# Two queues for the loads of the pairs' results, and the last four tiles in two groups

## The reference

```python
x = x + 0.5 * ffn(layernorm(x), Wg, W1, b1, W2, b2)
x = x + attn(layernorm(x), Wq, bq, Wk, bk, Wv, bv, Wo, bo)     # linear attention, 16 heads of 8
x = x + 0.5 * ffn(layernorm(x), Wg, W1, b1, W2, b2)

def ffn(x):                       # 8 experts, top 2 of them for each row
    top_w, top_i = top_k(x @ Wg, 2);  top_w = softmax(top_w)
    for i in range(8):
        out_i = gelu(x @ W1[i] + b1[i]) @ W2[i] + b2[i]        # 128 -> 512 -> 128
        results += w_per_expert[..., i:i+1] * out_i
```

## Time and profile before

| | us |
|---|---|
| median of 3 runs | 366.19 |
| lowest and highest of the 3 | 363.96, 366.23 |
| profiled execution | 364.38 |
| its span, first to last instruction | 362.6 |
| busy: PE, DVE, ACT, POOL | 306.7, 205.2, 148.7, 193.9 |
| mean granted clock of TensorE, 1 is 2.4 GHz | 0.928 |

### The profile page before, as it was taken

The page is one execution under the profiler, slowest core; times in us unless marked ns, Lnnn a source line. Parts: engine busy times, 40 slices in busy tenths (PEclk is TensorE's granted clock), DMA queues, the critical chain, the costliest instruction groups (busy, mean ns, idle before and its releaser), DMA issues.

```text
span 362.6 us, 7860 instructions
## 1 busy us (share of the span) xinstructions
PE 306.7 (85%) x2040; PEld 253.7 (70%) x2047; DVE 205.2 (57%) x562; ACT 148.7 (41%) x480; POOL 193.9 (53%) x246
## 2 busy tenths in 40 slices
PE   8589898759789995899999995895997777599985
PEld 6355898749779964566777763464997767499844
DVE  2974463333245516799999999972553242345413
ACT  3652675433244321434554552822764342343200
POOL 9307556656645531676677773236556656555500
PEclk9766999998889999999999998589999899989997
DMA  6937575534446126000000000226574535354146
GB/s 208 314 118 197 151 195 147 157 106 132 131 123 185 60 67 196 0 0 2 1 3 0 1 3 30 89 67 173 153 212 130 164 101 157 102 166 136 43 128 228
DMA packets 23557, 41.52 MB, mean 114 GB/s; under 512 B 4065, under 2 KB 6113, under 8 KB 23522
## 3 DMA queue, kind: packets, MB, share of 16 engines
q1 hardware_dynamic: 19426, 32.68, 31.6%
q0 software_dynamic: 4096, 8.40, 7.8%
HBM read 33.72 MB, written 7.34 MB: 113 GB/s over the span
## 4 chain that ended last, share of the span: by engine, by line
PE 48%; DVE 18%; another core or an unknown queue 12%; issue 5%; DMA 5%; ACT 5%; POOL 3%; DVEq 2%; SPq 0%; POOLq 0%; ACTq 0%
PE banks L1120 16%; PE banks L1129 14%; PE banks L1252 4%; DMA y_back<-y_rows 3%; DVE prod L967 2%; DVE local L971 2%; PE banks L1082 2%; PE banks L1138 2%; DMA y_rows<-y_back,pair_row 2%; PE banks L1228 2%; PE banks L1020 2%; ACT h_act L583 1%; POOL kv L464 1%; PE banks L1192 1%
## 5 line engine op out<-in xcount | busy, mean ns | idle before, releaser
L887 DVE TENSOR_TENSOR h_pre<-banks,w1b 128x512 f32<-128x512 f32 x78 | 53.7, 689 | 80.2 <-PE banks L1120 59.1
L433 POOL DMA_INDIRECT y_back<-xn_rows,src_row x64 | 61.9, 968 | 66.7 <-issue 20.3
L1120 PE MATMUL banks<-rows_sb,w1b 128*128 x624 | 88.6, 287 | 0.9 <-issue 0.6
L1129 PE MATMUL banks<-w,h_act 128*128 x624 | 85.6, 284 | 0.0
L441 POOL DMA_INDIRECT y_rows<-y_back,pair_row x64 | 62.6, 978 | 39.0 <-DVE y_back L899 27.9
L1120 PEld LDWEIGHTS banks<-rows_sb,w1b 128*128 128x128 f32 x624 | 79.8, 200 | 3.9 <-issue 2.0
L1129 PEld LDWEIGHTS banks<-w,h_act 128*128 128x128 f32 x624 | 79.7, 201 | 0.0
L583 ACT ACTIVATE h_act<-h_pre 128x512 f32<-128x512 f32 x78 | 48.8, 625 | 21.8 <-DVE h_pre L887 20.5
L575 ACT COPY rows_sb<-banks 128x128 f32<-128x128 f32 x64 | 16.7, 261 | 86.4 <-remote 57.4
L899 DVE SCALAR_TENSOR_TENSOR y_back<-banks,own_item,y_back 128x128 f32 x78 | 27.4, 351 | 34.0 <-PE banks L1129 18.0
L1138 PE MATMUL banks<-ident,y_back 128*128 128x128 f32 x64 | 18.7, 292 | 29.8 <-ACT rows_sb L575 25.3
(11 more groups left out here) (214 smaller groups left out, 426.1 us busy)
## 6 DMA issues: line engine op xcount, KB each, us to landing
w1b<-in_W1b SPq DMA_DIRECT2D x78, 258.0 KB
y_back<-y_rows SPq DMA_DIRECT2D x16, 256.0 KB, 5.3
xn_rows<-rows_sb SPq DMA_DIRECT2D x8, 256.0 KB, 2.6
rows_sb<-in_x_T SPq DMA_DIRECT2D x4, 256.0 KB, 3.7
x<-in_x_tiles SPq DMA_DIRECT2D x4, 256.0 KB, 6.1
y_back<-xn_rows,src_row POOLq DMA_INDIRECT x64
y_rows<-y_back,pair_row POOLq DMA_INDIRECT x64
out<-x SPq DMA_DIRECT2D x4, 256.0 KB, 2.4
```

The source lines that it names most:

```text
L433: g.indirect_dma_start(out=xg[:, n, :], out_offset=None, in_=xn_rows[f][:, :], in_offset=bass.IndirectOffsetOnAxis(ap=src_row[:, n:n + 1], ...
L887: v.tensor_tensor(h_pre[:, r, :].rearrange("p (c n) -> p c n", c=FC), h_bank(r).rearrange("p (c n) -> p c n", c=FC), w1b[:, q, DF:DF + FC] ...
L1120: last = mm(h_bank(r)[:, c * P:(c + 1) * P], w1b[:, q, c * P:(c + 1) * P], xgT[:, bass.ds(at[i][0], P)], start=True, stop=True)
L1129: last = mm(y_bank(r), h_act[:, r, c * P:(c + 1) * P], w2[:, bass.ds(col + c * P, P)], start=(c == 0), stop=(c == FC - 1))
```

## The change

The four k = 0 loads of a loop stay on SP; the four k = 1 loads are issued by ScalarE, which waits for `scattered` itself. In loop 1 the last group of four tiles (t = 12 to 15) becomes two groups of two tiles, each with a bank of its own (3 and 4), its own two loads of 128 KB, its own `mix` on TensorE, its own wait on VectorE and its own store of 128 KB. Loop 0 keeps its four groups. In the diff stand, one behind the other, the tables, the loads on SP, the stores, ScalarE's loads at the end of its `ffn(f)`, VectorE's `combine(f)` and TensorE's `mix_b2` and `mix`.

```diff
+    FOURS = tuple((c * CH, (c + 1) * CH) for c in range(NC))
+    GROUPS = (FOURS, (*FOURS[:-1], (NT - CH, NT - 2), (NT - 2, NT)))
...
-        def mix_bank(c): return banks[:, (1, 2, 0, 3)[c], :]
+        def mix_bank(c): return banks[:, (1, 2, 0, 3, 4)[c], :]
...
+        def loads(f, c):
+
+            return 16 * (f + 1 if c < NC else 1)
...
-                for c in range(NC):
-                    for k in range(TOPK):
-                        sp.dma_start(y_back[:, k, c * CH:(c + 1) * CH, :],
-                                     back_rows[k, :, c * CH:(c + 1) * CH, :]).then_inc(y_loaded[k][c], 16)
+                for c, (a, b) in enumerate(GROUPS[f]):
+                    sp.dma_start(y_back[:, 0, a:b, :], back_rows[0, :, a:b, :]).then_inc(y_loaded[0][c], 16)
...
-            for c in range(NC):
-                sp.wait_ge(x_final, CH * (c + 1))
-                sp.dma_start(out_v[:, c * CH:(c + 1) * CH, :], x[:, c * CH:(c + 1) * CH, :]).then_inc(out_stored, 16)
-            sp.wait_ge(out_stored, 16 * NC)
+            for a, b in GROUPS[1]:
+                sp.wait_ge(x_final, b)
+                sp.dma_start(out_v[:, a:b, :], x[:, a:b, :]).then_inc(out_stored, 16)
+            sp.wait_ge(out_stored, 16 * len(GROUPS[1]))
...
+                act.wait_ge(scattered, 16 * NL * (f + 1))
+                back_rows = y_rows[f].rearrange("(k p t) d -> k p t d", k=TOPK, p=P)
+                for c, (a, b) in enumerate(GROUPS[f]):
+                    act.dma_start(y_back[:, 1, a:b, :], back_rows[1, :, a:b, :]).then_inc(y_loaded[1][c], 16)
...
-                for c in range(NC):
+                for c, (a, b) in enumerate(GROUPS[f]):
                     dve.wait_ge(mix_ps, NC * f + c + 1)
-                    dve.wait_ge(y_loaded[1][c], 16 * (f + 1))
-                    for t in range(c * CH, (c + 1) * CH):
+                    dve.wait_ge(y_loaded[1][c], loads(f, c))
+                    for t in range(a, b):
...
+            def mix_b2(f, c):
+
+                a, b = GROUPS[f][c]
+                four = a // CH
+                rows = slice(four * CH * E, (four + 1) * CH * E)
+                mm(mix_bank(c)[:, 0:(b - a) * P], w_allT[rows, :], b2_blk[rows, (a % CH) * P:(a % CH + b - a) * P],
                    start=False, stop=False, skip_group_check=True)
 
             def mix(f, c):
-                pe.wait_ge(y_loaded[0][c], 16 * (f + 1))
-                for t in range(c * CH, (c + 1) * CH):
+                a, b = GROUPS[f][c]
+                pe.wait_ge(y_loaded[0][c], loads(f, c))
+                for t in range(a, b):
```

More of the change, by code:

```diff
@@ L259, in macaron_kernel @@
         y_ps, y_sb = map(sem, ("y_ps", "y_sb"))
-        y_loaded = [[sem(f"y_loaded{k}_{c}") for c in range(NC)] for k in range(TOPK)]
+        y_loaded = [[sem(f"y_loaded{k}_{c}") for c in range(len(GROUPS[1]))] for k in range(TOPK)]
         xa_sb, xa_ps, xaT_sb, qkv_ps = map(sem, ("xa_sb", "xa_ps", "xaT_sb", "qkv_ps"))
@@ L932, in moments_2 @@
                         v.bn_stats(stats[:, t, :], x[:, t, :]).then_inc(stats_ready, 1)
-                for c in range(NC):
+                for c, (a, b) in enumerate(GROUPS[f]):
                     dve.wait_ge(mix_ps, NC * f + c + 1)
-                    dve.wait_ge(y_loaded[1][c], 16 * (f + 1))
-                    for t in range(c * CH, (c + 1) * CH):
+                    dve.wait_ge(y_loaded[1][c], loads(f, c))
+                    for t in range(a, b):
                         v.scalar_tensor_tensor(out=x[:, t, :], in0=y_back[:, 1, t, :], scalar=half_w[:, 1, t:t + 1],
-                                               in1=mix_bank(c)[:, (t % CH) * P:(t % CH + 1) * P],
+                                               in1=mix_bank(c)[:, (t - a) * P:(t - a + 1) * P],
                                                op0=ALU.mult, op1=ALU.add).then_inc(x_final if f else x_mid, 1)
@@ L1093, in experts @@
                 pe.wait_ge(table_ready, f + 1)
-                mix_x(0)
+                mix_x(f, 0)
                 keep_warm(WARM_EXPERTS)
@@ L1169, in experts @@
                     pe.wait_ge(b2_in, 16)
[L1170 to L1173, removed]
+                mix_b2(f, 0)
+                for c in range(1, len(GROUPS[f])):
+                    mix_x(f, c)
+                    mix_b2(f, c)
                 pe.wait_ge(y_sb, base + NS)
@@ L1176, in experts, with mix_x @@
                 pe.wait_ge(diag_ready, NT * (f + 1))
-            def mix_x(c):
-                for t in range(c * CH, (c + 1) * CH):
[L1181 to L1186, removed]
+            def mix_x(f, c):
+                a, b = GROUPS[f][c]
+                for t in range(a, b):
+                    mm(mix_bank(c)[:, (t - a) * P:(t - a + 1) * P], ident[:, :], x[:, t, :],
+                       start=(t == a), stop=False, skip_group_check=True)
+            def mix_b2(f, c):
[3 more added lines that the diff above has]
+                mm(mix_bank(c)[:, 0:(b - a) * P], w_allT[rows, :], b2_blk[rows, (a % CH) * P:(a % CH + b - a) * P],
                    start=False, stop=False, skip_group_check=True)
             def mix(f, c):
-                pe.wait_ge(y_loaded[0][c], 16 * (f + 1))
-                for t in range(c * CH, (c + 1) * CH):
-                    last = mm(mix_bank(c)[:, (t % CH) * P:(t % CH + 1) * P], diag[:, t, :], y_back[:, 0, t, :],
+                a, b = GROUPS[f][c]
+                pe.wait_ge(y_loaded[0][c], loads(f, c))
+                for t in range(a, b):
+                    last = mm(mix_bank(c)[:, (t - a) * P:(t - a + 1) * P], diag[:, t, :], y_back[:, 0, t, :],
                               start=False, stop=True, skip_group_check=True)
@@ L1298, in _ @@
             experts(1)
-            for c in range(NC):
+            for c in range(len(GROUPS[1])):
                 mix(1, c)
```

## The result

The first measurement: 372.46 us for the changed kernel (370.9 to 375.29, 4 runs) against 366.21 (363.96 to 369.37, 4 runs). The ratio on record is 1.0227, 95% interval 1.0175 to 1.028; it is formed from fast runs alone and is not the quotient of the two medians, which is 1.017. So the change measured slower by about 2%, where 365.0 us and a range up to 367.2 had been forecast. The profiled execution took 375.29 us, its span is 373.5, the mean granted clock 0.895 (before: 364.38, 362.6, 0.928).

A forecast was written before the change was run, and what follows sets the result against it. Bound: result loads, on the chain twice with nothing beside them to fill the time. Terms +0.3 + 0.1 - 0.1 - 0.4 = -0.1 us, applied to the four executions' mean 365.2 and rounded, gave 365.0 us; range 361.8 to 367.2.

The forecast's parts named there:

- The loads' landings: Sign, loop 0: a pair landing together at 4.0 to 4.7 us after issue confirms that the queues share the service.
- Loop 0, +0.3 us with bounds -0.6 and +1.1: First pair in loop 0: both loads land together, TensorE's part stands uncovered, VectorE starts group 0 0.3 us later.
- Rival 1: Loads in both loops: the second queue speeds the service, -0.5 to -1.7 us, down to -2.2, about 363.0 us; chance 0.27.
- The end, +0.1 -0.1 -0.4: End of loop 1: group 2's pair order +0.1 us, last group in two -0.1, half-size last store -0.4.
- TensorE's clock in the last three groups: Sign at the end of loop 1, listed without a size; rival 1 said TensorE perhaps stays at full clock.
- The sum of -0.1 us: Whole program: +0.3 + 0.1 - 0.1 - 0.4 = -0.1 us, within -0.6 to +0.4; chance 0.45.
- rival 2: Group 0 in loop 0, group 2 at the end: TensorE's cover lost, nothing won, +0.5 to +1.4 us, about 365.3; chance 0.18.
- TensorE ahead of the loads: Last group's bias matmul, split in two halves: same sum, weight loads at worst 0.3 us, 0.49 us waiting to spare: no cost.
- slower by over 1% has no mechanism here: 0.02: Whole program: nothing in the change could slow it by over 1%; chance 0.02, against 0.86 for within 1%.
- shifts elsewhere, in TensorE's clock or in the gathers: Outside the changed places: shifts said to move the time by less than 1%; chance 0.02 together with rival 4.
- rival 4: ScalarE's issue, loop 0: late at its wait, k = 1 loads follow k = 0; each microsecond late costs one; chance shared, 0.02.

The follow-up runs named there:

- e9: The changed kernel without an edit, repeated in the third job: 326.0 us, ratio 0.999 to the kernel before.
- e10: The kernel before without an edit, in the third job: 325.85 us, ratio 0.9991.
- e8: The changed kernel without an edit, repeated in the second job: 326.25 us, ratio 1.0017 to the kernel before.
- e4: The kernel before without an edit, in the first job of the experiments: 363.38 us, ratio 0.9974.
- e18: The kernel before without an edit, in the fifth job: 325.47 us, ratio 1.0009.
- e1: The changed kernel without an edit, in the first job of the experiments: 364.84 us, ratio 1.0025 to the kernel before.
- e13: The changed kernel without an edit, in the fourth job: 326.62 us, ratio 0.9995 to the kernel before.
- e17: The changed kernel without an edit, in the fifth job: 325.59 us, ratio 0.9993 to the kernel before.
- e5: Changed kernel; in loop 1 TensorE also waits for five ScalarE copies between its last item and first bias matmul: 334.51 us, ratio 1.0294 to the kernel before.
- e6: Kernel before with the added TensorE wait of e5: 332.98 us, ratio 1.0231 to the kernel before.
- e14: e5 again, the changed kernel with the added wait, in a later job: 332.68 us, ratio 1.0234 to the kernel before.
- e16: Kernel before with only the second load queue (four groups of four in both loops), plus the wait of e5: 334.36 us, ratio 1.0252.
- e15: e6 again, the kernel before with the added wait, in a later job: 334.11 us, ratio 1.0238 to the kernel before.
- e7: e5 with twelve bf16 matmuls on zeros behind the added wait: 329.72 us, ratio 1.0138 to the kernel before.

## Why the prediction was wrong, point by point

**The loads' landings: right.** Forecast was a pair that lands together at 4.0 to 4.7 us. Measured 4.1 and 4.3, in e9 4.0 and 4.2 (loop 0) and 4.2 and 4.4 (loop 1). On one queue the first load alone was sooner. The first load of loop 1 in e10, then the first pair of loop 1 in e9:

```profile
y_back<-y_rows SPq DMA_DIRECT2D x1, 256.0 KB, 3.2
...
y_back<-y_rows SPq DMA_DIRECT2D x1, 256.0 KB, 4.2
y_back<-y_rows ACTq DMA_DIRECT2D x1, 256.0 KB, 4.4
```

**Loop 0, +0.3 us with bounds -0.6 and +1.1: right.** VectorE's first sum started 5.3 to 5.7 us after the first issue in the 13 traces with two queues, median 5.5, and 4.7 to 6.0 us in the 7 with one, median 5.2. That is +0.3 or +0.4. Single traces could not have told it: on one queue they differ by more than that among themselves.

**Rival 1, faster service with two queues (0.27): did not come.** Slow windows like those of the earlier trace rows are there with two queues too. Windows of e9 behind the first issue:

```profile
310.38:311.38 1.00, 1.00 (x7) 0.73 (x6) 0.00 (x0) 0.00 (x0) 0.00 (x0) 1.00 0.73 174
311.38:312.38 1.00, 1.00 (x5) 0.40 (x5) 0.00 (x0) 0.00 (x0) 0.00 (x0) 1.00 0.74 234
312.38:313.38 1.00, 0.46 (x3) 0.00 (x0) 0.00 (x0) 0.00 (x0) 0.00 (x0) 1.00 0.84 186
313.38:314.38 1.00, 0.68 (x6) 0.71 (x7) 0.00 (x0) 0.00 (x0) 0.00 (x0) 1.00 0.82 170
314.38:315.38 1.00, 0.45 (x5) 0.26 (x3) 0.51 (x2) 0.00 (x0) 0.00 (x0) 1.00 1.02 350
```

The rule that the prediction cited from the Trainium skill, "DMA: Bandwidth & Descriptors", section "Issuing engines are not separate DMA queues", holds here: two queues bring the last load in at the same 9.7 us as one.

**The end, +0.1 -0.1 -0.4: all three terms mis-sized, in opposite directions.** In e9 and e10 VectorE starts group 2 at 9.3 and 8.65 us behind the first issue: +0.7 us, not +0.1. From there to the end of its sums it takes 2.16 us and not 2.73: -0.6, not -0.1, as e10's VectorE waited 0.49 us ahead of its last group. The last store of 128 KB took 2.2 us, where 256 KB takes 2.3: -0.1 and not -0.4. That the sum comes out near the forecast in this pair is luck. With the other traces in which the clock stays up, first issue to end of program is 14.1 and 14.2 us changed (e9, e8) and 13.7, 13.8 and 14.1 before (e4, e18, e10): some 0.3 us later, where 0.4 sooner was forecast.

**TensorE's clock in the last three groups,** named as a sign, decides nothing. It fell there in three of the five later traces of the changed kernel (e1, e13, e17) and in one of the four of the kernel before, the first. First issue to end is then 14.6 to 15.1 us. These are too few traces to tell the two kernels apart.

**The sum of -0.1 us: not contradicted, and not confirmed to its size.** Five jobs, 60 executions of the changed kernel, ratios 1.0025, 1.0017, 0.999, 0.9995 and 0.9993, each with an interval of 0.3 to 0.45% to either side. Each alone tells no change within about 1.5 us; their mean is 1.0000. That leaves room for the forecast and for the lower part of rival 2 (+0.5 to +1.4 us), and the traces, +0.3 in loop 0 and about +0.3 at the end, lie between the two.

**What failed** are two sentences. The first, under "TensorE ahead of the loads", is "no cost". It took the bias and x matmuls at their length in the one trace (7.5 us, 8.5 with the zeros), with 0.49 us of waiting behind them to spare. At 1.2 GHz they are 14.7 us, the cover is gone, and all behind them moves. Measured in its place: 7.4 us behind the first issue in the first trace, 2.5 us of lost head start in it; 6.1 to 8.3 us when a wait was put there, the wait included. That this work can run at the lower clock could have been read from the earlier trace rows, where the last groups took 1.57 us instead of 1.13; the size could not, as here 1.12 us became 2.07.

The second is "slower by over 1% has no mechanism here: 0.02", and with it the upper end of the range. The prediction had "shifts elsewhere, in TensorE's clock or in the gathers" among its rivals, at 0.02 with rival 4, and said without a row for it that they move the time by less than 1%. They are open to both kernels and moved it by 2%. The profiled execution of the changed kernel stood in the state. For the other three there is only the mean clock: 0.894 and 0.904 are under the lowest of the 35 executions of the kernel before in the first job of the experiments (0.912), 0.916 is not, so for that one it is not shown. For the kernel before, the profiled execution was not in the state; the other four, 363.96 to 369.37 us, have neither clock nor trace.

**What stays open.** Why the first measurement met the state, and none of 60 later executions did as far as their times tell: none is more than 0.4 us above the slowest execution of the kernel before beside it. The trace shows a wait of TensorE right ahead of the stretch, and e5 and e6 show that such a wait suffices. What made TensorE wait can be followed one step. Waits of the changed kernel, 336 to 374 us, by waiting engine and releaser: sum of idle time in us, count, longest.

```profile
DVE h_pre L895 <- remote: 2.6, 1, 2.6
PE banks L1137 <- ACT h_act L587: 2.0, 1, 2.0
```

VectorE waited from 342.15 to 344.80 for something "remote", a releaser that the profile cannot name, and handed the delay on to ScalarE and TensorE. No load of weights or rows was under way then, only scatters of results. Such remote waits belong to the slower level of the times and not to the change: they are in all six traces at 360 us and over, of both kernels, and in none of the 14 at 325 to 336 us. Waits over the whole program in e4, the kernel before:

```profile
ACT rows_sb L575 <- remote: 52.9, 15, 5.6
DVE h_pre L887 <- remote: 17.2, 5, 6.2
```

A wait of TensorE ahead of its last item is in five of those six traces (1.96 us in the first one of the changed kernel; 0.87, 0.42, 0.41 and 0.87 in e1 to e4) and in none of the seven at the faster level that have no added wait. This weakens the repeats: 48 of the 60 executions ran in jobs whose traces show no wait of TensorE at that place. Only the 12 of e1 ran at the level of the first measurement. That the change makes the wait longer there is therefore not excluded; e1 and e4, with 0.87 us each, speak against it.

## What to carry to other kernels

The second queue brought the last load in no sooner (9.7 us after the first issue either way) and the first load 0.9 to 1.0 us later (4.0 and 4.2 against 3.1 and 3.2 in e9 and e10): it took the head start from the load that was needed first. Work that is hidden behind a transfer by less than its own length is hidden only at the clock at which it was seen: price it at 1.2 GHz as well, and look at what stands ahead of it, since behind a wait of 2 to 3 us it took nearly twice as long. Four executions in one job are not a measurement of one per cent when a state of 8 us exists; repeat in other jobs before the cause is sought in the code, and check by the traces that the repeats have the waits that the first measurement had.

## What the runs showed of the hardware

**A low clock that stays.** From the FP32 stretch (bias and x matmuls) into `mix` TensorE's row is nearly full, and still the granted clock stayed at 0.50 for 20.5 us in the first trace and in e5, 17.1 in e14 and e16, 13.7 in e6 and e15. In e7, with twelve bf16 matmuls on zeros ahead of the stretch, it was back at 1.0 before their 4.04 us were over. Which wait is followed by a fall is not settled by its length: the clock fell in `mix` behind a wait of 1.07 us in e13 and stayed up behind one of 1.63 us in e4.

**The same kernel at 363.8 us and at 325.4.** The kernel before took 363.83 us (35 executions) in the first job and 325.48, 326.36, 326.32 and 325.37 in the others. The difference lies in the two loops over items: from their first matmul to the start of the last 92.5 and 98.0 us in e4, 76.2 and 75.9 in e10, while the attention takes 68.3 and 68.5 (first to last prefix matmul). The view of the line where TensorE turns a gathered tile (1138): what ended its idle time, with sum in us and count, in e4 and then in e10:

```profile
  issue: 43.8, 26
  ACT rows_sb L575: 15.5, 8
```

```profile
  DMA y_back<-xn_rows,src_row: 6.8, 9
  issue: 1.0, 2
```

In e4 ScalarE waits 52.9 us in all for a releaser called remote ahead of its copies out of that line's bank, and in e10 never. What the remote releaser is, and whether the level comes from the chip or from its neighbours' traffic, these runs do not tell.
